# Edge stage of a two-layer graph network on one core: one broadcast compare per group for its end one-hots and one for its source one-hots, and a smaller store of A rows

## The reference

```python
h = jnp.maximum(_layernorm(x), 0.0)
x = x + sage(sage(h))          # two layers: mean over incoming edges @ W_l + x @ W_r + b, relu
h = jnp.maximum(_layernorm(x), 0.0)
# last layer, edge by edge
h_edge = jnp.concatenate([h[src], h[dst]], axis=-1)
m_ij = jax.nn.relu(h_edge @ W_interact + b_interact)
m_i = jax.ops.segment_sum(m_ij, src, num_segments=6250) / 4
out = x + h + jax.nn.relu((h + m_i) @ W_update + b_update)
```

## Time and profile before

| | |
|---|---|
| median of 3 runs | 2258.25 us (2257.73 to 2262.24) |
| the profiled execution | 2257.1 us |
| its span, first to last instruction | 2255.3 us |
| PE busy, matmuls | 1975.5 us (88%), 18416 instructions |
| DVE busy | 2007.2 us (89%), 7858 instructions |
| ACT busy | 1069.5 us (47%), 1192 instructions |
| POOL busy | 806.3 us (36%), 827 instructions |

### The profile page before, as it was taken

How to read it: one execution, slowest core, us unless ns; L and a number is a source line. 1 busy time by engine, 2 the same in 40 slices (tenths; PEclk the granted TensorE clock), 3 DMA queues, 4 the chain that set the end, 5 groups by cost and what they waited for, 6 DMA issues and landing times.

```text
span 2255.3 us, 52048 instructions
## 1 busy us (share of the span) xinstructions
PE 1975.5 (88%) x18416; PEld 1683.7 (75%) x18416; DVE 2007.2 (89%) x7858; ACT 1069.5 (47%) x1192; POOL 806.3 (36%) x827
## 2 busy tenths in 40 slices
PE   1508769999999889999999995379999999999997
PEld 1405447777787757777777784379999999999997
DVE  5969999999988489989989876379999999999997
ACT  1716446777777577777777753312111111121221
POOL 2346991000000000000000001267777777777774
PEclk9957999999999979999999996789999999999999
DMA  2000000000000000000000012335444444444443
GB/s 83 1 7 1 7 4 7 8 7 7 7 7 7 10 1 7 7 7 7 7 7 7 7 36 68 109 81 109 107 101 104 109 105 100 107 108 104 102 107 101
DMA packets 71082, 105.93 MB, mean 47 GB/s; under 512 B 13386, under 2 KB 51122, under 8 KB 70829
## 3 DMA queue, kind: packets, MB, share of 16 engines
q0 software_dynamic: 19264, 39.49, 9.9%
q1 hardware_dynamic: 49982, 62.55, 8.6%
q10 hardware_dynamic: 1584, 0.59, 0.1%
HBM read 92.26 MB, written 10.33 MB: 45 GB/s over the span
## 4 chain that ended last, share of the span: by engine, by line
DVE 43%; PE 43%; issue 4%; DMA 3%; SPq 2%; ACT 2%; POOL 2%; DVEq 1%; POOLq 0%; ACTq 0%
PE ps L902 31%; DVE slab L1526 13%; PE ps L892 10%; DVE hot L1284 6%; DVE ps L1542 4%; DVE tslot L1533 3%; DVE table L1520 3%; DVE rest L1533 3%; DVE table L1518 2%; POOL cells L630 2%; DVE hot L1278 1%; DMA cells<-b_rows,work 1%; SPq L481 1%; DVE slab L1181 1%; DVE stats L1081 1%
## 5 line engine op out<-in xcount | busy, mean ns | idle before, releaser
L719 ACT ACTIVATE slab<-ps 128x980 bf16<-128x980 f32 x626 | 786.2, 1274 | 350.7 <-PE ps L892 349.4
L902 PE MATMUL ps<-slab,table 128*128 128x320 bf16 (+1 forms) x5880 | 874.3, 296 | 0.0
L902 PEld LDWEIGHTS ps<-slab,table 128*128 128x128 bf16 x5880 | 568.8, 98 | 178.9
L630 POOL DMA_INDIRECT cells<-b_rows,work x600 | 574.1, 957 | 193.2 <-issue 187.5
L1284 DVE TENSOR_SCALAR hot<-iota_hi,cell_hi 128x246 bf16<-128x246 bf16 x2504 | 596.9, 308 | 0.0
L812 ACT ACTIVATE slab<-ps 128x384 f32<-128x384 f32 x300 | 147.4, 491 | 628.3 <-DVE ps L1542 625.2
L892 PE MATMUL ps<-hot 128*128 128x245 bf16 x2504 | 382.6, 278 | 71.1 <-DVE hot L1284 62.9
L617 POOL TENSOR_TENSOR tslot<-cells,slab 125x640 f32<-125x640 f32 x6 | 9.9, 1653 | 1089.5 <-DVE slab L1471 1089.5
L892 PEld LDWEIGHTS ps<-hot 128*128 128x128 bf16 x2504 | 269.8, 115 | 140.6 <-DVE hot L1284 80.1
L1015 PE MATMUL ps<-slab 125*128 125x128 bf16 x5496 | 357.7, 219 | 3.1 <-DVE slab L1526 1.0
L1278 DVE TENSOR_TENSOR hot<-iota_lo,cell_lo 128x512 bf16<-128x512 bf16 x626 | 268.0, 428 | 79.8 <-PE ps L892 77.8
(11 more groups left out here) (217 smaller groups left out, 1485.5 us busy)
## 6 DMA issues: line engine op xcount, KB each, us to landing
hot<-lane_d SPq DMA_DIRECT2D x50, 562.5 KB
cells<-b_rows,work POOLq DMA_INDIRECT x600
inv<-inv_row SPq DMA_DIRECT2D x40, 160.0 KB, 3.0
keys<-up_d SPq DMA_DIRECT2D x50, 93.8 KB
keys<-down_d SPq DMA_DIRECT2D x50, 93.8 KB
b_rows<-cells SPq DMA_DIRECT2D x10, 312.5 KB
a_rows<-table SPq DMA_DIRECT2D x10, 312.5 KB
out<-slab SPq DMA_DIRECT2D x9, 320.0 KB
```

The costliest lines, as they stand in the source:

```text
L630: p.indirect_dma_start(rows_g[:, gi % RS, j, :], None, b_rows, bass.IndirectOffsetOnAxis(ap=node_t[:, t:t + 1], axis=0)).then_inc(e_gath[g ...
L719: a.activation(slab[par][:, :, u * UB * BW:(u + 1) * UB * BW].rearrange("p h (k d) -> p k h d", k=UB), psum_unit(u).rearrange("p k (h d) - ...
L902: last = t.matmul(ps[:, 4 + par, 0:width], table[:, k // TERMS, k % TERMS, :], slab[par][:, k // TERMS, 0:width], start=k == 0, stop=k == ...
```

## The change

- `end_hot` of a group is made by one `tensor_tensor` over (windows x 128) elements: the row of numbers, repeated for each window, against `up_h` or `down_h`, f16, one number per window, repeated 128 times. `up_h` and `down_h` are made by iotas; `up_c` keeps one column.
- `src_hot` of a group is made by one `tensor_tensor` over 3 x 125 float elements. For it the lane numbers are laid out by groups in `lane_g`, which lies in the tile of the sorted keys, and the last three end tiles are taken in the order 15, 16, 17.
- The unpacking of the keys moves from ahead of the padding's memset to behind the norm's statistics, and ends in three small instructions that fill `lane_g`.
- SP stores the A rows only after all B rows, block by block, as many blocks as the general path's inner loop has trips: one here. The general path's node numbers are clamped to that block (124). At the start, SP copies x to `a_rows` (so that all of it is initialised) and waits for that copy ahead of its first fetch of `inv`.
- SP's wait ahead of the row stores is for the last built unit instead of the last dense product of the second layer.
- POOL reads the loop counts before it waits for the A rows.

```diff
-    END_TILES = (0, 1, 2, TB - 1, TB - 2, TB - 3)
+    END_TILES = (0, 1, 2, TB - 3, TB - 2, TB - 1)
...
+        lane_g = last_T[:, 0:NB * TB]
...
             rounds = rounds_of(sp)
+            sp.dma_start(a_rows, x[:, :]).then_inc(s_first, 16)
+            sp.wait_ge(s_first, 16)
...
-            sp.wait_ge(AS[1]["dense"], rounds * NS + PRE)
+            sp.wait_ge(AS[1]["built"], rounds * UNITS + LAG)
...
-                if c:
-                    sp.wait_ge(f_aok, c)
-                    sp.dma_start(a_rows[(c - 1) * CB:c * CB, :].rearrange("(t p) f -> p t f", p=BN),
-                                 a_kept[0:BN, (c - 1) * CT:c * CT, :]
-                                 ).then_inc(f_sta, 16)
             sp.wait_ge(f_aok, NC)
-            sp.dma_start(a_rows[(NC - 1) * CB:N, :].rearrange("(t p) f -> p t f", p=BN),
-                         a_kept[0:BN, (NC - 1) * CT:NC * CT, :]
-                         ).then_inc(f_sta, 16)
+            _, n_b = trips_of(sp)
+            with sp.Fori(0, n_b) as b:
+                sp.dma_start(a_rows[bass.ds(b * BN, BN), :].rearrange("(t p) f -> p t f", p=BN),
+                             a_kept[0:BN, bass.ds(b, 1), :]).then_inc(f_sta, 16)
...
-            pool.wait_ge(f_sta, 16 * NC)
-            n_t, _ = trips_of(pool)
+            n_t, n_b = trips_of(pool)
+            pool.wait_ge(f_sta, n_b * 16)
+            pool.sem_inc(s_past[0], 1)
...
+            v.tensor_scalar(gate[:, 3:4], gate[:, 1:2], float(N - BN), float(BN - 1), ALU.mult, ALU.add)
...
-            v.tensor_scalar(node_t.rearrange("p (k f) -> p k f", f=FH), by_tile, LANE, (1 << DSH) - 1,
-                            ALU.arith_shift_right, ALU.bitwise_and).then_inc(q_node, 1)
-            lane_ti = lane_t.bitcast(i32)
-            link(v.tensor_scalar(lane_ti.rearrange("p (k f) -> p k f", f=FH), by_tile, (1 << LANE) - 1, None,
-                                 ALU.bitwise_and))
-            link(v.tensor_scalar(lane_t, lane_ti, 1.0, gate[:, 2:3], ALU.mult, ALU.add))
...
             norm_stats(NS_[1])
+            v.tensor_scalar(node_t.rearrange("p (k f) -> p k f", f=FH), by_tile, LANE, (1 << DSH) - 1,
+                            ALU.arith_shift_right, ALU.bitwise_and).then_inc(q_node, 1)
+            link(v.tensor_scalar(lane_i.rearrange("p (k f) -> p k f", f=FH), by_tile, (1 << LANE) - 1, None,
+                                 ALU.bitwise_and))
+            dve.wait_ge(q_node, 1)
+            of_tile = lane_i[:, 0:NB * TB].rearrange("p (b t) -> p b t", t=TB)
+            to_group = lane_g.rearrange("p (b g j) -> p b g j", g=GB, j=GT)
+            for to, of in ((to_group[:, :, 0:SIDE, 0], of_tile[:, :, 0:SIDE]),
+                           (to_group[:, :, SIDE:GB, 0], of_tile[:, :, TB - SIDE:TB]),
+                           (to_group[:, :, :, 1:GT], of_tile[:, :, SIDE:TB - SIDE].rearrange(
+                               "p b (g j) -> p b g j", j=GPB))):
+                last = v.tensor_scalar(to, of, 1.0, gate[:, 2:3], ALU.mult, ALU.add)
+            link(last)
...
-                v.tensor_scalar(g_node[:, :], one, float(N - 1), None, ALU.min).then_inc(g_idx, 1)
+                v.tensor_scalar(g_node[:, :], one, gate[:, 3:4], None, ALU.min).then_inc(g_idx, 1)
...
-                numbers = up_c if end < SIDE else down_c
-                for w in range(w0, w1):
-                    last = v.tensor_scalar(end_hot[0:BN, gi % 4, w - w0, :], row, numbers[0:BN, w:w + 1], None,
-                                           ALU.is_equal)
+                numbers = (up_h if end < SIDE else down_h)[0:BN, w0:w1]
+                whole = [BN, w1 - w0, P]
+                last = v.tensor_tensor(out=end_hot[0:BN, gi % 4, 0:w1 - w0, :], in0=row.unsqueeze(1).to_broadcast(whole),
+                                       in1=numbers.unsqueeze(2).to_broadcast(whole), op=ALU.is_equal)
...
-                for j, tile in enumerate([end] + [SIDE + GPB * g + j for j in range(GPB)]):
-                    at = b * TB + tile
-                    last = v.tensor_scalar(src_hot[gi % 6][:, j, :], iota_w[:, 0:BN], lane_t[:, at:at + 1], None,
-                                           ALU.is_equal)
+                last = v.tensor_tensor(out=src_hot[gi % 6], in0=iota_w[:, 0:BN].unsqueeze(1).to_broadcast([P, GT, BN]),
+                                       in1=lane_g[:, gi * GT:(gi + 1) * GT].unsqueeze(2).to_broadcast([P, GT, BN]),
+                                       op=ALU.is_equal)
```

More of the change, by code:

```diff
@@ L536, in _ @@
             p.memset(share[:, :], float(CAP)).then_inc(s_iota, 1)
[L537 to L538 removed]
+            numbers(up_c[:, :], [[0, 1]], 1)
+            numbers(up_h[:, :], [[BN, 12]], 1)
+            p.iota(down_h[:, :], pattern=[[BN, 12]], base=BN - 1, channel_multiplier=-1,
                    allow_small_or_imprecise_dtypes=True).then_inc(s_iota, 1)
```

14 lines of the change are left out of this document (7 added, 7 removed).

## The result

The changed kernel takes **2354.07 us** (median of 6 runs, 2336.86 to 2362.76) where the kernel before takes 2257.99 (6 runs, 2254.77 to 2262.24): a ratio of 1.0409, 95% interval 1.0369 to 1.0449. It is 4.1% slower. The forecast was 2235 us with a range up to 2285; the time lies far above it, at the upper end (2358) of the rival "POOL's reads get blocked". The profiled execution took 2355.36 us, its span is 2353.6.

What follows compares the result with a forecast made beforehand. It took POOL's gathers as the edge stage's floor, level with DVE. Savings of 17 + 0.5 + 3 + 4 = 24.5, less 1, made 23 us: 2235 us, own range 2226 to 2246, full range 2226 to 2285.

Steps and rivals of the forecast that it cites:

- POOL's reads get blocked: Rival, edge stage: DVE compares with two SBUF inputs delay gathers' index reads, 0.20 us each; 2279, up to 2358; chance 0.26.
- the gathers settle into gaps: Milder case of blocked reads in the edge stage: about a third of 119 us, 40, less 18 for the entry: 2279.
- the compares' sizes: DVE, edge stage: source compare 0.46 us, end compare 0.87 on average; DVE saves 0.23 us per group.
- DVE didn't become the bound: Rival, edge stage: a dearer repeated operand makes DVE need 2.92 us per group; about 2350 us; chance 0.04.
- the steady part: Edge stage: POOL's gather pitch at best falls to 1.25 us, worth 4 us, and 3 us of slot waits go.
- The entry: Start of the edge stage: unpacking moved and A stores taken from SP's queue save 17 us, bounds 11 and 20.
- (a): Entry: key unpacking moves behind the norm statistics, so the first B part shifts earlier by the full 4.2 us.
- (b): Entry: ten A-row stores leave SP's queue, so DVE's last three B parts wait less: 7.6 us.
- (c): Entry, last B part to POOL's first gather: without A stores ahead of the last B store, 5.5 us go.
- (d): General path's gather, which waited 2.18 us for the last A store and loop counts: 0.5 us saved, ends 0 and 2.
- The copy of x: Copy to a_rows ahead of SP's first fetch of inv: 15 to 30 us, covered by 72 us less 3, so 0.
- the 0.06 for the entry: Rival chance that the entry doesn't shrink, PE, ScalarE and DVE passing chunks in turn: 2252, at worst no change; half level.

Runs made afterwards that it cites:

- the end compare alone: The changed kernel with only the end compare as a broadcast compare and the source compares single again: 2414.32 us, 1.0672 of the kernel before.
- the source compare alone: The changed kernel with only the source compare as a broadcast compare and the end compares single again: 2268.10 us, 1.0036 of the kernel before.
- PSUM operand: The changed kernel with both broadcast compares kept, one operand of each copied once into PSUM, so one SBUF input each: 2239.34 us, 0.9916 of the kernel before.

## Why the prediction was wrong, by its steps

**The step that failed** is the choice between forecast and rival: the forecast's sum puts the gathers' wait for their reads at nothing and their pitch at 1.25 us. As a rival the prediction had the mechanism, its place and its price: "a gather that starts at any point of the 2.5 us meets one of them and waits ... 0.20 us; 596 x 0.20 = 119 at most". Measured: 112.7 us more of gathers, 0.19 each. It gave this 0.26, and within it took "about a third if the gathers settle into gaps", 2279. Both were wrong. The reasons against it were "one per partition" and "today's short compares cost it nearly nothing". The first says how much a gather reads; the runs show that a hold lasts as long as the other instruction does. The second is no evidence: today's compares have one SBUF input. The row that did bear on it, L617 standing beside L1456, was of this kind. The settling into gaps was a hope without a row: a gather behind a held one starts 1.20 us behind the end of the hold, and what stands there in DVE's next group decides. With the end compare alone that was the compare again (0.32 us a gather, where the same price gives 0.15).

That 0.19 comes so close to 0.20 is in part luck. The price took the starts as evenly spread. That fits the source compare alone (24.7 us against the 25 expected) and failed for the end compare alone; in the changed kernel the gathers that start in step mostly pass just ahead of the end compare, and some are held through both.

**Right:** the compares' sizes. From start to start the source compare takes 0.46 us as forecast, an end compare of seven windows 1.00 and one of five 0.73, as the float rows give it (164 + 896 x 1.01 - 80 = 989 ns). DVE got some 0.28 us per group, a little more than the forecast 0.23: by the means over the stage, the compares of a group took 1.62 us before and 1.34 after. DVE didn't become the bound.

**Right:** POOL as the floor of the stage, against the chain's picture of DVE. It is the reason why DVE's gain was worth nothing, and why the hold cost in full. With the hold gone (PSUM operand) the kernel takes 2239.34, and my own range for the forecast case was 2226 to 2246.

**Mis-sized:** the steady part. "596 x 0.007 = 4 us" and 3 more of slot waits: from first to last of the 602 indirect transfers, general path included, the kernel before needs 763.4 us and the PSUM-operand version 759.8; 1.9 of the 3.6 are the general path's. So 1.7 instead of 7. (The upper bound of 8 us was also worked out too small: 1.257 less the 1.24 of its row is 0.017 and not 0.013, which gives 10.) POOL's slot waits are not fewer there: 20.4 us in 58 waits of 0.35, which now take the place of "issue" rather than add to it.

**The entry:** 13.7 us instead of 17, in the bounds 11 and 20. Some 0.5 us of it is no work of the change: DVE's last instructions of the layers already end that much earlier. The rows of after:

```profile
1391.15 0.82 DVE L1479 TENSOR_TENSOR cells<-ps,bias 125x640 f32<-125x640 f32 x1 [2.97 <-PE ps L982]
...
1411.01 0.82 DVE L1479 TENSOR_TENSOR cells<-ps,bias 125x640 f32<-125x640 f32 x1 [10.78 <-DMA b_rows<-cells]
...
1440.74 0.82 DVE L1479 TENSOR_TENSOR cells<-ps,bias 125x640 f32<-125x640 f32 x1 [1.36 <-PE ps L982]
...
1443.78 0.82 DVE L1479 TENSOR_TENSOR cells<-ps,bias 125x640 f32<-125x640 f32 x1 [1.49 <-PE ps L982]
...
1451.35 1.20 POOL L632 DMA_INDIRECT cells<-b_rows,work  x1 [1.74 <-issue]
```

(a) was priced at 4.2; the first B part comes at 1391.15, 2.9 earlier than 1394.01, since it now waits 2.97 us for PE. (a) and (b) together put the last B part at 1443.78, 8.7 earlier than before, not 11.8: the waits for stores in the last chunks are gone as forecast, but 1.36 to 1.49 us for PE stand there now. (c) from the last B part to the first gather 7.6 us instead of 12.6: 5.0 of the 5.5.

(d) The general path's gather no longer waits at all (2.18 us before): 1.9 against 0.5, at the upper end. The copy of x cost nothing, as forecast, and took less than forecast: SP issues it at 164.17 us and goes on at 176.77.

```profile
a_rows<-in_x SPq DMA_DIRECT2D x1, 3125.0 KB, 12.0
```

With 72 us of cover, 12 is as good as 30.

In the chances, half of the 0.06 for the entry was entered as 0.02 on one side and 0.04 on the other; nothing hung on it.

The sum from the measured parts: -13.7 of entry, -1.9 on the general path, +112.7 of gathers, is +97.1; the last gather starts at 2325.3 against 2228.4, +96.9.

## What to carry to other kernels

Before two DVE instructions are merged into a broadcast tensor-tensor, see where both its inputs lie and whether GpSimd reads SBUF meanwhile; an indirect gather counts as a reader here. If it does and GpSimd is the pacing engine, put one of the inputs in PSUM (here 2239 against 2354 us), or keep the single compares. And when one engine's instruction is held by another's in a loop, don't price the collision by chance meetings: the next instruction starts at a fixed distance behind the end of the hold (1.20 us here), so look at what the other engine does at that point of its next round.

## What was not expected of the hardware

- A hold that ends with the compare it started in ends with a spread of 0.003 us, 0.05 ahead of the start of the instruction that follows. But between two such instructions back to back some gathers are let through and others not; a gather of 0.945 us grew to 2.457.
- The two compares one behind the other cost less (2354) than the longer one alone (2414): 0.13 us less between the end of a hold and the next end compare outweighs the second held stretch.
- Chips differ by 10% on the same kernel (2258 and 2260 us on two of them, 2494 and 2496 on two others), in one stage only: the first gather of the PSUM-operand version comes at 1450.1 on one and at 1452.7 us on another. The sign of an edit's worth changed with the chip.
